# Graph attention on one core: finished nodes attended inside the edge loop

## The reference

```python
Q = (x @ WQ).reshape(N, H, dh); K = (x @ WK).reshape(N, H, dh); V = (x @ WV).reshape(N, H, dh)
Eh = (edge_attr @ WE).reshape(-1, H, dh)
score = K[src] * Q[dst] / jnp.sqrt(jnp.float32(dh)) * Eh
score = jnp.exp(jnp.clip(score.sum(-1, keepdims=True), -5.0, 5.0))
wV = jax.ops.segment_sum(V[src] * score, dst, num_segments=N)
Z = jax.ops.segment_sum(score, dst, num_segments=N)
h = x + (wV / (Z + ATTN_EPS)).reshape(N, D)
mean, var = h.mean(axis=0), jnp.mean((h - h.mean(axis=0)) ** 2, axis=0)
y = (h - mean) * jax.lax.rsqrt(var + BN_EPS) * bn_gamma + bn_beta
return _layernorm(x + y, axis=-1)
```

## Time and profile before

| | us |
|---|---|
| median of 3 runs | 2390.87 (2381.74 to 2391.33) |
| the profiled execution | 2380.56 |
| its span in the trace | 2378.7 |
| busy: PE / DVE / ACT / POOL | 1785.9 / 1619.8 / 659.7 / 1665.9 |
| mean granted TensorE clock | 0.713 |

### The profile page before, as it was taken

One profiled execution on the slowest core, in us unless ns is written; L12 is line 12 of the kernel. 1 busy time (PEld: TensorE's weight loads), 2 busy tenths in 40 slices (PEclk: granted clock), 3 DMA queues, 4 the chain that ended last, 5 costly groups with the idle time before them and its releaser, 6 DMA issues.

```text
span 2378.7 us, 48811 instructions
## 1 busy us (share of the span) xinstructions
PE 1785.9 (75%) x14106; PEld 1636.8 (69%) x14106; DVE 1619.8 (68%) x3798; ACT 659.7 (28%) x1501; POOL 1665.9 (70%) x1718
## 2 busy tenths in 40 slices
PE   8777777778777787777777877777877777776763
PEld 8666767677667776676776766676767776666752
DVE  5587677666667666766666766676666666666368
ACT  2432222222222222222222222222222222222126
POOL 0557777777777777777777777777777777777243
PEclk9898677766677767767767677767677767777555
DMA  9955555555555555555555555555555555556102
GB/s 371 350 169 169 161 164 164 163 159 158 163 164 159 163 163 161 164 158 158 162 158 167 158 162 162 163 158 163 160 161 162 160 162 163 163 158 206 38 10 99
DMA packets 213520, 391.12 MB, mean 164 GB/s; under 512 B 93585, under 2 KB 94481, under 8 KB 211942
## 3 DMA queue, kind: packets, MB, share of 16 engines
q0 software_dynamic: 79728, 217.82, 32.1%
q1 hardware_dynamic: 133750, 172.85, 23.0%
HBM read 355.21 MB, written 28.88 MB: 161 GB/s over the span
## 4 chain that ended last, share of the span: by engine, by line
POOL 64%; issue 21%; PE 5%; DVE 5%; DMA 3%; ACT 1%; DVEq 0%; SPq 0%; ACTq 0%; POOLq 0%
POOL ring L376 64%; PE ohT_ps L639 2%; DMA q_rows<-ring 2%; PE qe_ps L649 1%; DVE ymr L919 1%; DVE ystat L901 1%; ACT ea L489 1%; PE ohT_ps L534 1%; DMA ring<-kv_rows,src_t 1%; PE qe_ps L534 1%; DVE z_sum L895 0%; PE eh_ps L534 0%; DVE kq L832 0%; DVE ssum L835 0%; DVE kq L826 0%
## 5 line engine op out<-in xcount | busy, mean ns | idle before, releaser
L376 POOL DMA_INDIRECT ring<-kv_rows,src_t x1661 | 1602.9, 965 | 595.7 <-issue 504.5
L610 PE MATMUL agg_ps<-onehot,ring 128*128 128x42 f32 x3328 | 592.6, 342 | 488.5 <-DVE ring L732 473.5
L610 PEld LDWEIGHTS agg_ps<-onehot,ring 128*128 128x128 f32 x3328 | 563.5, 256 | 553.2 <-DVE onehot L803 530.7
L600 PE MATMUL eh_ps<-we_sb,ea 128*128 128x128 f32 x3328 | 672.6, 367 | 0.0
L826 DVE TENSOR_TENSOR kq<-ring,qe_ps 128x512 f32<-128x512 f32 x416 | 285.6, 687 | 540.6 <-DMA ring<-kv_rows,src_t 528.0
L600 PEld LDWEIGHTS eh_ps<-we_sb,ea 128*128 128x128 f32 x3328 | 601.8, 271 | 0.0
L457 ACT ACTIVATE score<-sclip 128x32 f32<-128x32 f32 x416 | 95.4, 229 | 1363.0 <-DVE sclip L837 1348.4
L832 DVE TENSOR_TENSOR kq<-kq,eh_ps 128x512 f32<-128x512 f32 x416 | 285.8, 687 | 49.7 <-PE eh_ps L600 2.0
L443 ACT CAST onehot_b<-onehot 128x504 bf16<-128x504 f32 x416 | 254.2, 611 | 179.0 <-DVE onehot L803 178.7
L835 DVE TENSOR_REDUCE ssum<-kq 128x32 f32<-128x512 f32 x416 | 285.4, 686 | 14.4
L732 DVE TENSOR_TENSOR ring<-ring,score 128x512 f32<-128x512 f32 x416 | 285.0, 685 | 0.1
(11 more groups left out here) (94 smaller groups left out, 759.7 us busy)
## 6 DMA issues: line engine op xcount, KB each, us to landing
ea<-in_edgeT SPq DMA_DIRECT2D x416, 256.0 KB
ring<-kv_rows,src_t POOLq DMA_INDIRECT x1661
q_win<-q_rows SPq DMA_DIRECT2D x416, 31.5 KB
kv_rows<-ring SPq DMA_DIRECT2D x24, 512.0 KB, 8.1
q_rows<-ring SPq DMA_DIRECT2D x24, 384.0 KB, 5.1
z_sum<-acc SPq DMA_DIRECT2D x6, 1024.0 KB, 5.6
out<-z_sum SPq DMA_DIRECT2D x24, 256.0 KB, 2.0
z_sum<-in_xT SPq DMA_DIRECT2D x4, 1024.0 KB, 12.4
```

The costliest lines, as they stand in the source:

```text
L376: pool.indirect_dma_start(out=kv[:, s, j, :], out_offset=None, in_=kv_rows, in_offset=bass.IndirectOffsetOnAxis(ap=src_t[:, n * TILES + j: ...
L600: last = pe.matmul(eh_ps[s % 2][:, j * P:(j + 1) * P], ea[:, s, j * P:(j + 1) * P], we_sb[:, :], start=True, stop=True)
L610: pe.matmul(agg_ps[:, 0:WIN], kv[:, s, j, D:KV], onehot[:, s % 4, j, :], start=(j == 0), stop=(j == TILES - 1))
```

## The change

- **Q by blocks.** Only the first two blocks of 480 nodes are projected ahead of the loop, between chunks 1 and 2 of the projection. In each turn PE projects one further block (`project_q`, at u = 1), ACT and DVE split it (u = 2 to 5), and SP stores it (u = 14). The separate Q stage and the copies of zeros are gone; x is first loaded into `acc`.
- **Turns of 16 groups.** `SLOTS` is 16 for gathers; edge features and Q windows have 8 buffers (`EARS`).
- **Moving score sums.** The sums of scores are held only for the nodes in reach, in `z_live` (1,162 columns). In each turn, after u = 9, DVE moves them down by a block: two copies (480 and 202 columns) and a clear (`move_z`). The first node of each group is bounded to that range on the chip.
- **Finished nodes in the loop.** In turn t, the block t - 1 is attended: PE turns its sums (`turn_z`, u = 7), ACT, DVE, ACT (u = 8, 9, 10), PE turns back (u = 12), DVE multiplies (u = 13), adds x (u = 14, formerly POOL) and collects statistics (u = 15). SP loads x and `z_far` for it at u = 8. `z_far` in DRAM holds score sums of stray edges; SP fills it with zeros from `acc` before it loads anything for the loop.
- **Rows of the last chunk.** The projection's last chunk has 212 nodes. It was stored as 128 partitions of 2 rows (with padding), and is now stored as 53 partitions of 4 rows.
- **Last stage.** 26 blocks. ACT scales and shifts, POOL adds x, PE multiplies with `centre` (identity minus 1/128), which turns and takes out each node's mean in one product; ACT squares, DVE sums (`y_variance`), ACT takes the root, DVE the reciprocal and the product. POOL starts this stage when all 13 pieces of x have landed in `ring`, which SP loads as slots come free, behind `load_finished` of the last block.

```diff
-SLOTS = 8
+SLOTS = 16
+EARS = 8
+HEAD = 3
 NB = 512
+BLK = 480
+LAG = 5
+SHIFT = 9
+REACH = 640
...
-            return table[c * NB:c * NB + j * P, :].rearrange("(p j) d -> p j d", j=j)
+            return table[c * NB:c * NB + nodes_of(c) * TILES, :].rearrange("(p j) d -> p j d", j=TILES)
...
+                sp.dma_start(rows_of(kv_rows, c), kv[0:parts, s, :, :]).then_inc(kv_stored[s], 16)
+                if c in (4, 5):
+                    sp.wait_ge(q_lo, c - 3)
+                    sp.dma_start(q_block((c - 4) * BLK), q_st[0:BLK // TILES, c - 4].rearrange("p j k d -> p j (k d)")).then_inc(q_stored, 16)
+            sp.wait_ge(acc_clear, CHUNKS)
+            sp.dma_start(z_far, acc[0:HEADS, 0:N]).then_inc(z_zeroed, 16)
+            sp.wait_ge(z_zeroed, 16)
...
+            def load_finished(t, n0, size):
+
+                sp.wait_ge(h_done, t)
+                sp.dma_start(xs[:, 0:size], xT[:, ds(n0, size)]).then_inc(fin_landed, 16)
+                sp.wait_ge(z_turned, t)
+                sp.dma_start(z_add[:, 0:size], z_far[:, ds(n0, size)]).then_inc(fin_landed, 16)
+
+            def edge_turn(t):
+                turn = t if isinstance(t, int) else None
                 for u in range(SLOTS):
+                    if u == 0:
+                        sp.wait_ge(q_stored, 16 * (t + 2) if turn != TURNS - 1 else 16 * (TURNS + 1))
+                        if turn != TURNS - 1:
+                            if turn != 0:
+                                sp.wait_ge(q_ready, t + 2)
+                            sp.dma_start(xq[:, :], xT[:, ds(t * BLK + 2 * BLK, BLK)]).then_inc(xq_landed, 16)
+                    if u == 8 and turn != 0:
+                        load_finished(t, t * BLK - BLK, BLK)
                     load_edges(t, u)
-                    load_window(t, u)
-
-            sp.dma_start(xT_late[:, XRING:NPAD], xT[:, XRING:NPAD]).then_inc(late_landed[SLOTS], 16)
-            for u in range(SLOTS):
+                    load_range(t, u)
+                    if u == 14 and turn != TURNS - 1:
+                        sp.wait_ge(q_lo, t + 3)
+                        sp.dma_start(q_block(t * BLK + 2 * BLK), q_st[0:BLK // TILES, 0].rearrange("p j k d -> p j (k d)")).then_inc(q_stored, 16)
+
+            edge_turn(0)
+            with sp.Fori(1, TURNS - 1) as t:
+                edge_turn(t)
+            edge_turn(TURNS - 1)
+
+            load_finished(TURNS, (TURNS - 1) * BLK, LASTB)
+            for u in range(PIECES):
                 sp.wait_ge(agg_ready, NG - SLOTS + u + 1)
-                sp.dma_start(xT_late[:, u * PIECE:(u + 1) * PIECE], xT[:, u * PIECE:(u + 1) * PIECE]).then_inc(late_landed[u], 16)
-
-            for c in range(CHUNKS):
-                s, parts = c % 4, nodes_of(c)
-                sp.wait_ge(o_done, c + 1)
-                sp.dma_start(out[c * NB:c * NB + parts * TILES, :].rearrange("(p j) d -> p j d", j=TILES), o_rows[0:parts, s]).then_inc(out_stored[s], 16)
+                lo, hi = u * PIECE, min(N, (u + 1) * PIECE)
+                sp.dma_start(xT_late[:, lo:hi], xT[:, lo:hi]).then_inc(late_landed[u], 16)
...
-            for k in range(HN):
-                pool.wait_ge(att_done, k + 1)
-                for u in range(k * HC // PIECE, min((k * HC + HC - 1) // PIECE, SLOTS) + 1):
-                    pool.wait_ge(late_landed[u], 16)
-                h = acc[:, k * HC:(k + 1) * HC]
-                nc.gpsimd.tensor_tensor(h, h, xT_late[:, k * HC:(k + 1) * HC], ALU.add).then_inc(h_done, 1)
-
-            for c in range(CHUNKS):
-                pool.wait_ge(y1_done, c + 1)
-                if c >= 4:
-                    pool.wait_ge(yT_ready, c - 3)
-                nodes = nodes_of(c) * TILES
-                nc.gpsimd.tensor_tensor(y_sum[:, c % 4, 0:nodes], y_one[:, c % 2, 0:nodes], xT_late[:, c * NB:c * NB + nodes], ALU.add).then_inc(y_done, 1)
+            for u in range(PIECES):
+                pool.wait_ge(late_landed[u], 16)
+            for k in range(TURNS):
+                pool.wait_ge(y1_done, k + 1)
+                if k >= 4:
+                    pool.wait_ge(yT_ready, k - 3)
+                size = size_of(k)
+                nc.gpsimd.tensor_tensor(y_sum[:, k % 4, 0:size], y_one[:, k % 2, 0:size], xT_late[:, k * BLK:k * BLK + size], ALU.add).then_inc(y_done, 1)
...
+            def norm_nodes(k):
+                act.wait_ge(bn_step, 5)
+                if k >= 2:
+                    act.wait_ge(y_done, k - 1)
+                size = size_of(k)
+                nc.scalar.activation(y_one[:, k % 2, 0:size], acc[:, k * BLK:k * BLK + size], ACT.Identity, scale=bn[:, 4:5], bias=bn[:, 6:7]).then_inc(y1_done, 1)
+
+            def square(k):
+                parts = size_of(k) // TILES
+                act.wait_ge(yT_ready, k + 1)
+                if k >= 2:
+                    act.wait_ge(yvar_done, k - 1)
+                nc.scalar.activation(y_sq[0:parts, k % 2, :], yT_ps[k % 4][0:parts, :], ACT.Square).then_inc(ysq_done, 1)
+
+            def y_std(k):
+                parts = size_of(k) // TILES
+                act.wait_ge(yvar_done, k + 1)
+                nc.scalar.activation(ystd[0:parts, k % 4, :], ysq[0:parts, k % 4, :], ACT.Sqrt, bias=eps_ln[0:parts, :], scale=1.0 / D).then_inc(ystd_done, 1)
+
+            for k in range(2):
+                norm_nodes(k)
+            for k in range(TURNS):
+                square(k)
+                if k + 2 < TURNS:
+                    norm_nodes(k + 2)
+                y_std(k)
...
+                if c == 1:
+                    pe.wait_ge(wq_scaled, 1)
+                    for k in range(2):
+                        project_q(q_ps[k], xT_early[:, k * BLK:(k + 1) * BLK], BLK)
...
+            def turn_z(t, added, parts):
+                pe.wait_ge(fin_landed, 32 * t)
+                pe.wait_ge(agg_added, added)
+                for j in range(TILES):
+                    to = zT_ps[0:parts, j * HEADS:(j + 1) * HEADS]
+                    pe.matmul(to, z_live[0:ZROWS, j * parts:(j + 1) * parts], gather8[0:ZROWS, :], start=True, stop=False)
+                    last = pe.matmul(to, z_add[:, j * parts:(j + 1) * parts], ident[0:HEADS, 0:HEADS], start=False, stop=True)
+                last.then_inc(z_turned, 1)
+
+            def turn_back(t, parts):
+                pe.wait_ge(zw_done, t)
+                for j in range(TILES):
+                    quarter = z_wide[0:parts, j * HEADS:(j + 1) * HEADS, :].rearrange("p h d -> p (h d)")
+                    last = pe.transpose(aux_ps[:, j * parts:(j + 1) * parts], quarter, ident[0:parts, 0:parts])
+                last.then_inc(rT_turned, 1)
...
+                    if u == 1 and turn != TURNS - 1:
+                        pe.wait_ge(xq_landed, 16 * (t + 1))
+                        project_q(aux_ps, xq, BLK)
+                    if turn != 0:
+                        if u == 7:
+                            turn_z(t, t * SLOTS + LAG, QP)
+                        if u == 12:
+                            turn_back(t, QP)
+                    sum_range(t, u)
...
-                    last = pe.transpose(yT_ps[s][0:parts, j * P:(j + 1) * P], y_sum[:, s, j:parts * TILES:TILES], ident[:, :])
+            edge_turn(TURNS - 1)
+            turn_z(TURNS, NG, LASTB // TILES)
+            turn_back(TURNS, LASTB // TILES)
+
+            for k in range(TURNS):
+                s, size = k % 4, size_of(k)
+                pe.wait_ge(y_done, k + 1)
+                if k >= 4:
+                    pe.wait_ge(o_done, k - 3)
+                for j in range(TILES):
+                    last = pe.matmul(yT_ps[s][0:size // TILES, j * P:(j + 1) * P], y_sum[:, s, j:size:TILES], centre[:, :], start=True, stop=True)
...
+            def move_z(t):
+                dve.wait_ge(agg_added, t * SLOTS + SHIFT)
+                dve.wait_ge(z_turned, t + 1)
+                nc.vector.tensor_copy(z_live[0:ZROWS, 0:BLK], z_live[0:ZROWS, BLK:2 * BLK]).then_inc(z_moved, 1)
+                dve.wait_ge(z_moved, 3 * t + 2)
+                nc.vector.tensor_copy(z_live[0:ZROWS, BLK:ZW - BLK], z_live[0:ZROWS, 2 * BLK:ZW]).then_inc(z_moved, 1)
+                dve.wait_ge(z_moved, 3 * t + 3)
+                nc.vector.memset(z_live[0:ZROWS, ZW - BLK:ZW], 0.0).then_inc(z_moved, 1)
+                dve.wait_ge(z_moved, 3 * t + 4)
+
+            def z_reciprocal(t, parts):
+                dve.wait_ge(z_shifted, t)
+                nc.vector.reciprocal(z_rec[0:parts, :], z_eps[0:parts, :]).then_inc(zr_done, 1)
+
+            def attend(t, n0, size):
+                dve.wait_ge(rT_turned, t)
+                m = acc[:, ds(n0, size)]
+                nc.vector.tensor_tensor(m, m, aux_ps[:, 0:size], ALU.mult).then_inc(att_done, 1)
+
+            def add_x(t, n0, size):
+                dve.wait_ge(att_done, t)
+                h = acc[:, ds(n0, size)]
+                nc.vector.tensor_tensor(h, h, xs[:, 0:size], ALU.add).then_inc(h_done, 1)
+
+            def measure(t, n0, size):
+                dve.wait_ge(h_done, t + 1)
```

(40 more changed lines are left out.)

668 lines of the change are left out of this document (303 added, 365 removed).

## The result

The changed kernel takes 2296.03 us (median of 4 runs, 2294.21 to 2302.56), the kernel before 2387.75 (4 runs beside it). The ratio is 0.9623, 95% interval 0.9593 to 0.9653: 90 us faster. 2285 was forecast, with 2262 to 2312 as the range. Eight of the runs further down were taken while the chips ran slower, with the kernel before at 2779 to 2780 us beside them; the gathers do not set the pace there, so of these runs I read the gathers' length and the ramps, and compare their times only among themselves.

What follows compares the result with a forecast made beforehand. POOL's gather stream was taken to bound the kernel, with ramps around it. Terms 12.6 - 33.3 + 8 + 0.8 - 80.4 - 5.8 = -98.1 us took 2380.56 to 2282.5; forecast 2285, range 2262 to 2312.

Steps and rivals of the forecast that it cites:

- First gather: Before the loop: two added Q blocks and a 53-partition store on one engine start the first gather 12.6 us later.
- Stall: POOL's one wait for full slots before the loop: sixteen slots remove it, -33.3 us.
- The stream: POOL's gathers in the loop: DVE's new operations lengthen them, +8 us, from 0 to 51.
- the formula's 13: Gathers in the loop: new DVE operations meeting gather starts at random cost 0.54 us a turn, 13 us in 25.
- rival A: Gathers in the loop are lengthened more, by DVE's additions and copies: up to 51 us, 2328 us in all; chance 0.10.
- Ramp at the end: Last gather to last stage: last sum +0.8 us, then one block's attention instead of 25 rounds, -80.4 us.
- the forecast's second chain: Before the last stage: SP moves x, 6.4 MB, after block 24's addition; it lands 11 to 12 us after the last sum.
- Last stage: Final stage: a ring over two blocks paces it at 2.33 us a block; 69.1 us in all, -5.8 us.
- Rival C: The last stage runs at PE's throughput, 1.88 us a block: -11 us, 2274 us in all; chance 0.15.
- B: The last store lands sooner, spread over engines: -8 us, 2277 us in all; chance 0.10.
- D: PE becomes the loop's pace, slower than before: 177 us for half the loop, 2462 us in all; chance 0.03.
- E: DVE's in-order work in the loop is not covered and gathers wait behind it: +124 us, 2409; chance 0.02.

Runs made afterwards that it cites:

- experiment 3: Changed kernel with the last store of kv_rows cut into 48 and 5 partitions; 2717.45 us, with the kernel before at 2780.
- again: The changed kernel run again, unedited; 2294.84 us, ratio to the kernel before 0.9606.
- d_psum: Changed kernel plus one 128x512 product per group, one input from PSUM, one from SBUF; 2731.08 us, in its second run 2309.60 us.
- d_two: Changed kernel plus one 128x512 product per group, both inputs from SBUF; 2719.70 us, in its second run 2394.47 us.
- the combined kernel: Changed kernel with two operations reading one PSUM input, last kv_rows store cut, scaling three blocks ahead, x pieces asked for earlier; 2683.93 us, in another run 2274.02 us.
- experiment 4: Changed kernel with ACT scaling three blocks ahead in the last stage, not two, with four rooms; 2710.05 us, with the kernel before at 2780.

## Why the prediction was right, and where not

**First gather.** Right in its mechanism: 53 partitions on one engine, shown by experiment 3. The first gather started at 69.38 and not 71.9; 2.5 us of the term are too much.

**Stall.** Right: 16 slots cover the later start of the loop.

**The stream.** This is the term that was mis-sized: +8 was taken, +22.5 measured. The excess, all gathers' time over 946 ns, rose from 31.6 to 53.2 us; that is 21.6 of the 22.5, and the pauses between the gathers hold the other 0.9. By the operation that ended last over each gather's start (many gathers take 942 to 945 ns, hence the small negative rest):

| operation | before | after |
|---|---|---|
| weighing | 28.4 | 43.8 |
| addition of x (25 in the loop) | | 3.9 |
| lowest part of Q (before: ahead of the loop) | 1.4 | 2.9 |
| one-hot | 2.4 | 2.5 |
| copies | | 0.3 |
| others and scatter | -0.6 | -0.2 |

The operations that the prediction priced cost 7.1 us: the addition of x spanned 12 starts, the lowest part of Q 14, the copies 11. That is near the +8 taken and about half of the formula's 13, as the prediction had it. The step that failed is the one that the sum had no term for: what the new work does to the old weighing. It spanned about as many starts as before (201 and 202 as the last to end), but held each of them for 0.22 us in the mean and not 0.14, 15.4 us more. Against rival A the prediction said that DVE starts from landed rows, which holds the phase. It does so in groups for whose rows DVE waits: 388 of the 416 before, 299 now, 174 in d_psum's second run, where the weighing's excess was 59.6 us. That added work alone can move the phase at the weighing's cost is shown by that run, whose added product holds nothing itself. That the fewer waits are what moves it is not shown: d_two's second run has 230 of them and 91.0 us. What sets the phase stays open. The trace of `again` has the same picture, with 48.5 us for the weighing and 8.5 for the new operations, so two executions of one kernel differ by 6 us in this term. A mean gather of 978 ns is also outside the 967 to 975 that were named as a sign of being right.

**Ramp at the end.** 24.3 us from the last gather to POOL's first addition, 24.0 forecast (12.5 and 11.5). POOL waited for pieces of x, as the forecast's second chain had it, not for the statistics: ACT had begun to scale the first block at 2221.40. So one of the signs named as wrong, POOL's additions held by pieces of x, did come, for the first addition: it started 2.5 us after ACT's scaling, where it starts 1.0 us after it in the combined kernel, which asks for x earlier.

**Last stage.** 2.38 us a block against 2.33, and the last store took the span's last 4.6 us against 4.7, so its 256 KB did not go at the 25 GB/s of one engine, which would be some 10 us. Rival C, PE's throughput, did not come true, and experiment 4 shows why: the look-ahead, not PE, was short. With one more block ahead the stage does run at PE's throughput, 1.76 us a block against the 1.88 of the forecast.

**Rivals A, B, D, E.** A is what happened in part, with 978 ns: 14.5 of its 43 us, but under the old weighing and not under DVE's additions and copies, where it was placed. B did not occur: the store took one engine's time. D did not occur: PE waited 317.5 us in front of its sums. E did not occur: DVE waited 258.2 us for gathered rows.

## What to carry to other kernels

Where a stream of indirect gathers sets the pace, look at every VectorE operation that reads both inputs from SBUF, or copies within it, as a tax on the stream: up to 0.5 us for one of 0.7 whenever it lies over a gather's start, and nothing if one input comes from PSUM. Price what added work does to the old operations too: here an unedited operation cost 15 us more because it lay otherwise against the gathers, twice what the new ones cost themselves. Both stores of 53 partitions here went through one engine; at a boundary that others wait for, cut such a store, here in 48 and 5 for 8 us. In a pipeline over several engines, add up the ring over the look-ahead and compare it with the busiest engine; here one more block ahead was worth 15 us.

## What the runs showed of the hardware

- The hold by phase (d_two, second run; product of 0.69 us): begun 0.1 us before the gather, 44 gathers took 1.41 us in the mean; 0.2 before, 1.31; 0.3 before, 1.20; 0.4 before, 1.10; 0.5 before, 1.01. Begun 0.1 to 0.7 us after the start: 0.95. The gather goes on when the operation ends: the excess is the operation's end less a point about 0.13 us behind the gather's start (0.69 - 0.1 - 0.13 = 0.46 of the first row).
- Reductions (0.69 us, one input in SBUF) were the last to end over 181 gathers' starts in the changed kernel, and none of these took more than 0.95 us. No gather of that trace started under a clear, so of clears nothing is shown. The clip, a short operation within SBUF, was itself slowed by the gather, as the earlier trace rows showed (0.34 us in the mean when begun 0.6 us into one, 0.18 when begun 0.1 to 0.4 us into it), and did not slow it.
- In the eight runs with the kernel before at 2779 to 2780 us the granted clock of TensorE in the loop was 0.63 to 0.66, where the changed kernel had 0.73 (400 to 2000 us), and the kernel of experiment 4 took 6.06 us a group in the mean and not 5.13. VectorE and GpSimd waited at the place where they wait for the window sums. In this stretch of the kernel of experiment 4 the last of these products ends at 1002.71 by the profile, and the addition that waits for it starts at 1006.02:

```profile
1002.45 0.26 PE L682 MATMUL agg_ps<-onehot,score 128*8 128x42 f32 x8
...
1003.51 0.18 DVE L955 TENSOR_SCALAR sclip<-ssum 128x32 f32<-128x32 f32 x1
...
1006.02 0.20 DVE L903 TENSOR_TENSOR acc<-acc,agg_ps 128x42 f32 x1 [2.33 <-remote]
```

Why the signal came 3.3 us after that end, and why the kernels took so much longer, is open.
